# State sum of a selective scan: identity matmuls replaced by accumulating transposes, with all places in the program drawn anew

## What is computed

```python
u, res = split(xn @ in_proj_w.T, 2)               # 256 + 256 channels
u_c = silu(causal_conv(u))                        # 4 taps
delta = softplus(dt_r @ dt_w.T + dt_b)            # dt_r, B, C = u_c @ x_proj_w.T
h = exp(delta * A) * h + (delta * u_c) * B        # a scan over tokens, 16 states
y = sum over the 16 states of h * C + u_c * Dp
y = y * silu(res)
out = y @ out_proj_w.T + x
z = gelu(out @ ff_w1.T + ff_b1) @ ff_w2.T + ff_b2 + out     # then a layer norm
```

## Time and profile before

| | us |
|---|---|
| median of 3 runs | 2152.82 |
| lowest, highest | 2145.71, 2153.9 |
| profiled execution | 2153.84 |
| its span, first to last instruction | 2152.1 |
| granted TensorE clock, mean | 0.893 |

### The profile page before, as it was taken

One profiled execution on the slowest core, in us unless ns is written; L12 is line 12 of the kernel. 1 busy time (PEld: TensorE's weight loads), 2 busy tenths in 40 slices (PEclk: granted clock), 3 DMA queues, 4 the chain that ended last, 5 costly groups with the idle time before them and its releaser, 6 DMA issues. The chain is left out here.

```text
span 2152.1 us, 23261 instructions
## 1 busy us (share of the span) xinstructions
PE 1668.6 (78%) x6097; PEld 925.3 (43%) x6186; DVE 1724.8 (80%) x4157; ACT 1547.5 (72%) x3340; POOL 1356.2 (63%) x1209
## 2 busy tenths in 40 slices
PE   4887878787888988887878879787878886755563
PEld 2333435354444445454544445454534443443342
DVE  3888989798988989898988899898989897733331
ACT  4566767587878978787878779787978775555443
POOL 0225454577676777677776767677677777566554
PEclk8899998999998999998999999998999898877766
DMA  2001111122222232222322222222323222233222
GB/s 55 0 10 50 39 57 33 52 74 81 77 76 80 76 87 71 82 74 66 93 79 77 76 73 77 84 72 70 84 77 83 79 76 79 71 87 94 79 81 71
DMA packets 79876, 150.76 MB, mean 70 GB/s; under 512 B 20584, under 2 KB 46592, under 8 KB 79680
## 3 DMA queue, kind: packets, MB, share of 16 engines
q0 software_dynamic: 49152, 134.28, 22.0%
q1 hardware_dynamic: 29344, 14.65, 2.4%
q10 hardware_dynamic: 1248, 0.34, 0.1%
HBM read 145.01 MB, written 4.19 MB: 69 GB/s over the span
## 5 line engine op out<-in xcount | busy, mean ns | idle before, releaser
L1453 POOL DMA_INDIRECT rows<-in_experts,index x1024 | 981.1, 958 | 461.6 <-issue 370.2
L1347 DVE TENSOR_TENSOR_SCAN hp<-dA,fed_ps 128x1024 f32<-128x1024 f32 x256 | 582.3, 2275 | 3.4 <-DVE fed_ps L1331 0.5
L773 PE MATMUL ysum<-hp,ident 128*128 128x512 f32 x1024 | 496.3, 629 | 16.5 <-DVE hp L1357 11.8
L1468 POOL TENSOR_TENSOR hp<-hp,c_row 128x1024 f32<-128x1024 f32 x112 | 263.9, 2356 | 254.0 <-ACT c_row L1037 152.2
L1331 DVE TENSOR_TENSOR fed_ps<-du,b_ps 128x1024 f32<-128x1024 f32 x256 | 312.7, 1222 | 45.7 <-PE b_ps L748 27.6
L1020 ACT ACTIVATE dA<-delta,decay 128x511 f32<-128x511 f32 x512 | 334.5, 710 | 11.5 <-issue 6.8
L999 ACT ACTIVATE rows<-rows,coef 128x128 f32<-128x128 f32 x1024 | 310.9, 390 | 22.1 <-DVE coef L1268 21.9
L1261 DVE CUSTOM_DVE_ANT_0 rows<-rows,xn 128x128 f32<-128x128 f32 x1024 | 268.1, 324 | 62.6 <-DMA rows<-in_experts,index 62.3
L773 PEld LDWEIGHTS ysum<-hp,ident 128*128 128x128 f32 x1024 | 211.0, 207 | 246.1 <-issue 209.0
L923 ACT ACT_TABLE_LOAD x218 | 279.7, 1283 | 8.8 <-PEq L533 4.9
L706 PE MATMUL bank<-rows,ident 128*128 128x256 f32 x1024 | 249.6, 400 | 32.7 <-ACT rows L999 31.1
(11 more groups left out here) (183 smaller groups left out, 2323.7 us busy)
## 6 DMA issues: line engine op xcount, KB each, us to landing
rows<-in_experts,index POOLq DMA_INDIRECT x1024
x_in<-in_x SPq DMA_DIRECT2D x16, 256.0 KB
x_res<-in_x SPq DMA_DIRECT2D x16, 256.0 KB
y<-x SPq DMA_DIRECT2D x16, 256.0 KB
rows<-in_taps SPq DMA_DIRECT2D x1, 512.0 KB
rows<-in_wq_t SPq DMA_DIRECT2D x1, 512.0 KB, 4.9
rows<-in_in_proj_t ACTq DMA_DIRECT2D x1, 256.0 KB
rows<-in_key_t SPq DMA_DIRECT2D x1, 128.0 KB, 5.1
```

The lines of the kernel that those rows point to most:

```text
L773: mm = nc.tensor.matmul(ysum[:, j, :], ident[:], hp[:, BUFFER[k], j, :], start=(k == SUM_ORDER[0]), stop=(k == SUM_ORDER[-1]))
L1347: nc.vector.tensor_tensor_scan(flat, dA[:, n % NDA, :, :].rearrange("p a b -> p (a b)"), fed_ps[:].rearrange("p a b -> p (a b)"), 0.0, ALU ...
L1453: pool.indirect_dma_start(e.rows[:, t, h, :], None, A["experts"], bass.IndirectOffsetOnAxis(ap=e.index[:, t, h:h + 1], axis=0)).then_inc(e ...
L1468: pool.tensor_tensor(state, state, c_row[:, k % NCR, :].unsqueeze(1).to_broadcast([P, NH, T]), ALU.mult).then_inc(pool_read, 1)
```

## The change

The state sum is formed token-major. For each state, eight matmuls in transpose mode, one for each 128 x 128 block of hp, put the block's transpose into ysum and add to what is there; hp is the stationary operand and the identity moves. ysum is seen as `by_token`, four token tiles of 256 channels. The skip is added with u_c stationary and w_skip moving, and the residual half of the convolution comes out token-major as well, so DVE's gating multiply stays one instruction; its result goes to the second half of ucs. A new step `pe_back` turns the gated product back by eight transposes into ysum, `act_back` copies it into the first half of ucs, and `pe_out` and the next batch's first sum wait for that copy.

All stages' places are redrawn: SLOTS changes, and LAST_SLOTS and FIRST_SLOTS give way to BATCH_SLOTS, places by batch for batches 0, 11 and 12 to 15. The places are cut here; the drain's fetches and the steps named are kept.

```diff
 SLOTS
+    "pe_back": (POST, (0,)),
     "pe_out": (POST, (0,)),
-    "pe_ff1": (POST, (1,)),
-    "pe_ff2": (POST, (6,)),
-    "pe_ln_a": (POST, (8,)),
+    "pe_ff1": (POST, (5,)),
+    "pe_ff2": (POST, (7,)),
+    "pe_ln_a": (POST, (10,)),
-    "pe_sim_e1": (POST, (35, 38, 44, 46)),
+    "pe_sim_e1": (POST, (35, 38, 45, 46)),
-    "pe_sim_e2": (POST, (177, 179, 182, 184)),
+    "pe_sim_e2": (POST, (177, 179, 182, 185)),
+    "act_back": (POST, (2,)),
     "act_out": (POST, (3,)),
-    "pool_fetch_e1": (POST, (43, 43, 47, 47, 61, 61, 61, 62)),
-    "pool_fetch_e2": (POST, (201, 202, 208, 217, 217, 217, 227, 228)),
+    "pool_fetch_e1": (POST, (40, 40, 50, 50, 62, 62, 62, 67)),
+    "pool_fetch_e2": (POST, (200, 203, 205, 219, 219, 219, 226, 229)),
...
-LAST_SLOTS = {
...
-    "pool_fetch_e1": (POST, (43, 43, 47, 48, 61, 61, 61, 62)),
-    "pool_fetch_e2": (POST, (196, 196, 205, 205, 214, 215, 224, 224)),
+BATCH_SLOTS = {
+    0: {
+        "pe_skip": (47,),
+        "act_keep_x": (63,),
+        "act_silu": (21, 30),
+        "act_exp": (63,),
+        "act_ln": (63,),
+        "pool_delta": (63,),
+    },
...
+    12: {
+        "pool_fetch_e1": (40, 42, 43, 51, 51, 61, 63, 67),
+        "pool_fetch_e2": (192, 195, 213, 227, 230, 232, 238, 238),
...
+    13: {
+        "pool_fetch_e1": (37, 43, 47, 47, 47, 63, 63, 63),
+        "pool_fetch_e2": (206, 208, 221, 222, 226, 227, 231, 242),
...
+    14: {
+        "pool_fetch_e1": (31, 39, 42, 45, 56, 57, 66, 70),
+        "pool_fetch_e2": (182, 185, 193, 197, 197, 199, 202, 229),
...
+    15: {
+        "pool_fetch_e1": (35, 39, 44, 46, 52, 61, 72, 83),
+        "pool_fetch_e2": (177, 199, 206, 214, 214, 221, 223, 241),
...
 def due(stage, i, q, slot):
+    phase, own = SLOTS[stage]
+    for m in range(NB):
+        for k, place in enumerate(BATCH_SLOTS.get(m, {}).get(stage, own)):
+            if (m - OFFSET[phase] + place // TURN, place % TURN) == (i, slot):
+                yield m, m % 2, k
...
+        by_token = ysum[:].rearrange("p j (t d) -> p (j t) d", d=DI)
...
                         if n == 1 and later(c):
-                            pe.wait_ge(y_gated, at(c - 1, 1))
+                            pe.wait_ge(y_back_sb, at(c - 1, 1))
                         for k in [x for x in SUM_ORDER if SUM_AT[x] == n]:
                             pe.wait_ge(*multiplied(c, k))
-                            for j in range(NH):
-                                mm = nc.tensor.matmul(ysum[:, j, :], ident[:], hp[:, BUFFER[k], j, :],
-                                                      start=(k == SUM_ORDER[0]), stop=(k == SUM_ORDER[-1]))
+                            for t in range(NT):
+                                for j in range(NH):
+                                    opens = k == SUM_ORDER[0] and j == 0 and t % HALF == 0
+                                    mm = nc.tensor.matmul(by_token[:, t, j * P:(j + 1) * P],
+                                                          hp[:, BUFFER[k], j, t * P:(t + 1) * P], ident[:],
+                                                          start=opens, stop=(k == SUM_ORDER[-1]),
+                                                          is_transpose=True, skip_group_check=True)
                             mm.then_inc(y_sum, 1)
                     for m, r, _ in due("pe_skip", i, q, slot):
                         pe.wait_ge(silu_done, at(m, 2, 0))
+                        for t in range(NT):
+                            for j in range(NH):
+                                nc.tensor.matmul(by_token[:, t, j * P:(j + 1) * P], ucs[r][:, j, t * P:(t + 1) * P],
+                                                 w_skip[:, j, :], start=False, stop=False, skip_group_check=True)
+                    for m, r, _ in due("pe_back", i, q, slot):
+                        pe.wait_ge(y_gated, at(m, 1))
+                        gated = ucs[r][:, NH:2 * NH, :].rearrange("p j (t d) -> p (j t) d", d=DI)
                         for j in range(NH):
-                            nc.tensor.matmul(ysum[:, j, :], w_skip[:, j, :], ucs[r][:, j, :], start=False, stop=False)
+                            for t in range(NT):
+                                mm = nc.tensor.transpose(ysum[:, j, t * P:(t + 1) * P],
+                                                         gated[:, t, j * P:(j + 1) * P], ident[:])
+                        mm.then_inc(y_back, 1)
...
-                            mm = nc.tensor.matmul(bank[0][:], w_res[:, (k - NH) * P:(k - NH + 1) * P],
-                                                  xrT[:, NK - 1:NK - 1 + T], start=True, stop=True)
+                            for t in range(HALF):
+                                first = NK - 1 + ((k - NH) * HALF + t) * P
+                                mm = nc.tensor.matmul(bank[0][:, t * DI:(t + 1) * DI], xrT[:, first:first + P],
+                                                      w_res[:], start=True, stop=True, skip_group_check=True)
...
                     for m, r, _ in due("pe_out", i, q, slot):
                         claim(1, i)
-                        pe.wait_ge(y_gated, at(m, 1))
+                        pe.wait_ge(y_back_sb, at(m, 1))
...
+                    for m, r, _ in due("act_back", i, q, slot):
+                        act.wait_ge(y_back, at(m, 1))
+                        nc.scalar.activation(ucs[r][:, 0:NH, :], ysum[:], ACT.Copy).then_inc(y_back_sb, 1)
...
-                    nc.vector.tensor_tensor(ucs[q][:, 0:NH, :], ysum[:], ucs[q][:, NH:2 * NH, :],
+                    nc.vector.tensor_tensor(ucs[q][:, NH:2 * NH, :], ysum[:], ucs[q][:, NH:2 * NH, :],
                                             ALU.mult).then_inc(y_gated, 1)
```

More of the change, by code:

```diff
@@ L96 @@
     "act_rstd_a": (POST, (6,)),
[L97 to L99 removed]
+    "act_rstd_e1": (POST, (16,)),
+    "act_norm_e1": (POST, (19,)),
+    "act_turn_e1": (POST, (31,)),
     "act_flip_e1": (POST, (41, 49)),
[L101 to L113 removed]
+    "act_gelu_e1": (POST, (64, 83)),
+    "act_scale_e1": (POST, (74, 76, 88, 91)),
+    "act_out_e1": (POST, (93, 97)),
+    "act_rstd_b": (POST, (102,)),
+    "act_norm_b": (POST, (106,)),
+    "act_turn_b": (POST, (120,)),
+    "act_xp": (POST, (125,)),
+    "act_gate": (POST, (125,)),
+    "act_tanh": (POST, (128,)),
+    "act_rstd_c": (POST, (141,)),
+    "act_rstd_e2": (POST, (161,)),
+    "act_norm_e2": (POST, (174,)),
+    "act_turn_e2": (POST, (175,)),
     "act_flip_e2": (POST, (181, 194)),
[L115 to L117 removed]
+    "act_gelu_e2": (POST, (223, 238)),
+    "act_scale_e2": (POST, (229, 233, 241, 246)),
+    "act_out_e2": (POST, (238, 255)),
     "dve_stats_x": (PRE, (0,)),
@@ L129 @@
+    "dve_stats_b": (POST, (100,)),
+    "dve_shift_b": (POST, (106,)),
     "dve_scan_b": (POST, (127,)),
     "dve_x3": (POST, (148,)),
[L131 to L135 removed]
+    "dve_stats_e2": (POST, (154,)),
+    "dve_shift_e2": (POST, (173,)),
+    "dve_top_e2": (POST, (179, 180, 183, 184)),
+    "dve_index_e2": (POST, (181, 200)),
@@ L228, in summed @@
     return SUM_ORDER.index(n)
-def offset(phase, slot):
-    return OFFSET[phase] - slot // TURN
 def due(stage, i, q, slot):
-    phase, slots = SLOTS[stage]
-    if i == -1 and stage in FIRST_SLOTS:
-        slots = FIRST_SLOTS[stage][1]
-    last = i >= LATE and stage in LAST_SLOTS
-    for k, own in enumerate(slots):
-        new = LAST_SLOTS[stage][1][k] if last else own
-        both = last and i == LATE and new // TURN < own // TURN
-        for x in (own, new) if both else (new,):
-            o = offset(phase, x)
-            assert -DEPTH <= o <= OFFSET[phase] and new // TURN <= own // TURN
-            if x % TURN == slot and 0 <= i + o < NB:
-                yield i + o, (q + o) % 2, k
+    phase, own = SLOTS[stage]
[3 more added lines that the diff above has]
+                yield m, m % 2, k
 def at(b, per, k=0):
```

396 lines of the change are left out of this document (286 added, 110 removed).

## The result

| | us |
|---|---|
| after, median of 4 runs | 2287.39 |
| after, lowest, highest | 2284.44, 2292.57 |
| before, measured beside it | 2153.36 |
| after to before | 1.0632, 95% interval 1.0598 to 1.0665 |
| after, profiled execution; its span | 2285.55; 2283.8 |

The change makes the kernel 6% slower, where I had forecast 2% faster. First the stretches, in the columns of the earlier trace rows: the middle from the fourth gating multiply on (11 iterations), the last full iteration, the drain.

The account below looks back on a forecast made before the run. DVE was taken to pace the middle, though not alone: it idles 11.7 us of each 118.8 us iteration, mostly awaiting PE. Forecast: 2153.8 - 30 (middle's waits) - 3 (first intervals) - 14 (drain) = 2106.8 us; range 2060 to 2175.

Parts of the forecast that it names:

- Bound and place of the waits: Middle: DVE sets the pace, busy 107.1 of 118.8 us an iteration; nearly all its idle time awaits PE.
- the three groups named: DVE's waits for PE in the middle: top reduce 77.6 us, fed multiply 18.0, bits shift 13.4; 9.9 an iteration.
- unknown wait: Part of the top reduce's wait in the middle, releaser unknown to the profile: 39.7 us, 3.6 an iteration, taken as unmoved.
- Price of the sum: State sum on PE, per batch: 64 records of 27.4 us go, 128 transposes of 14.1 us come.
- Relief of PE: PE in the middle: 12.4 us less per batch, busy time from 99.5 to 87.1 us an iteration.
- Waits shrink as PE's free time grows: Middle: DVE's waits shrink by 0.4 of 6.3 us, 2.5 an iteration, 30 us over 12 intervals.
- The new wait: pe_out waits for ACT's copy, moving 1.3 us; covered with 0.4 us to spare: cost 0, about 13 if uncovered.
- New places in the middle at 0: Middle: most stages move one to five slots and issue the same instructions, so the redrawn places cost 0.
- Drain -14: Drain: interleaving batch 15's first expert fetches with batch 12's second removes two gaps in POOL's queue, 14 us.
- Fill: First three intervals, where half the stages don't run yet: 1 us faster each, 3 in all.
- no relief: Rival, chance 0.25: the top's waits are a chain, not load; middle stays, 2140 to 2154 us, say 2147.
- The clock falls: Rival, chance 0.20: in the middle transposes don't keep PE's clock up; at 0.76 granted the kernel takes 2182 us.

Follow-up runs that it names:

- transposes alone: Kernel before with only the state sum's 64 matmuls exchanged for 128 transposes, nothing turned back: 2187.4 us, ratio 1.0173.
- the pieces: Kernel before with each 512-column matmul of its state sum cut into four of 128, identity still as weights: 2222.6 us, ratio 1.0322.
- the sum alone: Kernel before, its tables of places kept, with after's state sum, skip, residual half and turning back: 2237.7 us, ratio 1.0343.
- the common places: Kernel before, old sum, with after's SLOTS for all batches but before's first-batch and end places: 2179.9 us, ratio 1.0121.
- own places: BATCH_SLOTS of batches 0 and 11 to 15; kernel after with before's FIRST_SLOTS, LAST_SLOTS and `due` instead: 2193.8 us, ratio 1.0169 to before.

## Why the prediction was wrong

Two steps failed, and each outweighs what went right. DVE's waits were to shrink by 30 us over the middle and the last interval, as PE got less to do; the middle grew by 55 us and the last interval by 24. The drain was to be 14 us shorter, and it grew by 59. In place of the relief stand the short records of the sum, which lengthen the waits (37 us with the transposes alone), and two terms that I put at 0: the way back (44 us) and the new places.

- **Bound and place of the waits**: right. DVE sets the pace, and its waits for PE, in the three groups named, decide. The unknown wait I set aside as unmoved was the one that counted: of DVE's 109 us in the earlier trace rows, 52.8 have that releaser; with the transposes alone it is 94.6 of 141.3, with the pieces 115.2 of 167.0.
- **Price of the sum**: right. Eight records in 1.04 us, 0.109 apart in a stream; the sum's busy time fell by 12.2 us a batch, where I had 13.3 less.
- **Relief of PE**: 12.4 forecast, 99.5 - 94.8 = 4.7 found. The back's eight records take 1.6 us an iteration, and the projection 3.3 where it took 2.0. The other 4.6 are in PE's other groups, in a middle with 0.88 granted where it was 0.93.
- **Waits shrink as PE's free time grows**: this step failed. PE has more free time and DVE waits longer. In the two runs that have the sum's records alone changed, the pieces (+69 at unchanged columns) and the transposes alone (+37 with less to do), it waits more for the unknown releaser (115.2 and 94.6, was 52.8), and more of PE's announcements come late (173 and 151, was 123). So there DVE waits in good part not for PE's load but for the moment of its announcement. In after itself the number of late ones didn't grow; its loss in the middle is what the sum alone costs, less what the common places give back. My choice of a ratio with ends at 0 and +9.9 had no end on the side of a loss; the middle went to +55.
- **The new wait, cover 0.4 us, 13 if it is gone**: the local order was right (the projection starts 2.3 us behind the gate, 1.2 before, and state 2's fed multiply is not what waits), the cost was not: 44 us. What I left out is that PE stands still for the copy and that the projection behind it then takes 3.75 us instead of 1.98. That this makes the 44 us is argued; no run has the one without the other.
- **New places in the middle at 0**: failed, 26 us with the old sum, with waits of the bits for PE at 75.7 where they were 13.4. With the new sum they give back 38 (1.0343 - 1.0169), 15 either way. I had read that stages move by one to five slots, and not what stands between the one that makes and the one that waits.
- **Drain -14**: failed, +59, and +24 in the interval before. I priced POOL's queue and left out when the indices are made; the 8.4 us that POOL waits for them in the earlier trace rows became 120.9. The own places are the cause: without them both stretches are as before (280.6 and 125.0). Which of them is not shown.
- **Fill**: 6.5 us faster, forecast 3. That this came out is luck as far as is shown: the sum alone leaves the fill as it was.
- **The rivals**: "no relief" had the right doubt (the unknown wait) and the wrong end, none. "The clock falls" had the sign of the result, but not its mechanism. The Trainium skill, "TensorE: Matmul & The Clock Gate", Part 4 (PE-mode transpose), says that a transpose doesn't count as activity for the clock; here the trace disagrees, with 1.00 granted through 512 of them. In the middle 0.88 was granted, above the 0.80 at which I had it decide, and the pieces lose 69 us at 0.94.

Together: the sum with the way back 74 us, the common places -38 with it, the own places 100: 136, by the ratios. These are differences of runs in a chain, so that they add up says nothing by itself. No version tried beats the kernel before.

## What to carry to other kernels

An engine that is made less busy doesn't hand its time on by itself: read what its consumer waits for (the announcement, with semaphore times beside the records), and treat a wait with unknown releaser as a resource that the change may touch. In this kernel, which gathers most of the time, the number of short PE instructions was a cost of its own; halving the columns while doubling the records may lose. Tables of places that were drawn together are to be tested in parts, the fill, the middle and the end apart, each with the work they were drawn for.

## What the runs showed of the hardware that I had not expected

- PE's semaphore updates beside indirect gathers: with transposes streaming in groups of eight they are on time for two to four groups, then up to 26 us behind the records (28 with short bf16 matmuls), until the gathers end. Ten multiplies on POOL, or 4 MB of plain loads beside 11 of the 14 us, don't do that. In the kernel before, all 119 updates over 1 us late belong to records that end while gather packets move.
- An eighth of the rows in each gather doesn't help: 2363.8 us, and 192 late updates instead of 119.
- Accumulating fp32 transposes of 128 columns start 109 ns apart, like the records of fp32 matmuls (112; a matmul makes two), and 512 of them in a row run at a granted clock of 1.00.
- Beside DVE's multiplies of 1.2 us, each answering a group, gathers are issued more slowly: six in 8.3 to 10.1 us where they took 7.5.
